# Two adapter and feed-forward layers on one core: 8-bit integers carried as signed fp16 multiples of 2^-24 in place of offset 16-bit integers

## The chip, the cores and the metric

The kernel runs on one core of one Trainium2 chip. The metric is the time of one execution on the device, in microseconds (us), lower is better. The engines are called as the profile calls them: PE is TensorE (PEld its weight loads), DVE is VectorE, ACT is ScalarE, POOL is GpSimd, SP is SyncE, which only issues DMAs here. Each engine works off its own queue in order, and the queues are tied together by semaphores.

## What is computed

x is 8 batches x 512 tokens x 256 channels. Two layers follow each other, both with a residual:

```python
x = x + ffn0(cond0(x, itok_B_0_8))     # adapter of the batch's language, LayerNorm, gamma, beta
x = x + ffn1(cond1(x, itok_B_0_7))     # linear layer of the batch's subject

def bitlinear(x, W, b):                # both feed-forward parts use it twice, 256 -> 1024 -> 256
    w_scale = clip(mean(abs(W)), 1e-5)
    Wq = clip(round(W / w_scale), -1, 1) * w_scale                 # ternary weights
    x_scale = clip(max(abs(x), axis=-1), 1e-5)                     # per token
    xq = clip(round(x * (127 / x_scale)), -128, 127) * (x_scale / 127)
    return xq @ Wq.T + b

ffn0 = bitlinear(gelu(bitlinear(x, W1, b1)), W2, b2)
ffn1 = bit_linear(silu(depthwise_conv1d(bit_linear(x, w1), conv_w, conv_b)), w2)   # conv over 3 tokens
```

So four times per token a row is divided by its own largest magnitude, rounded to integers within -127 to 127, and multiplied by a matrix of -1, 0 and 1. The product is an exact integer sum, and the two scales are multiplied in afterwards.

## The kernel before

**Tiling.** A batch is four tiles of 128 tokens (two pairs). All loops are unrolled. The queue of each engine is an order written out by hand: `first()` holds the first layer for all batches and the beginning of the second, `slot2(s)` repeats for the steady part of the second layer (one batch of it per slot), and `ending()` closes. No queue is sorted by anything else, so an instruction that is late holds up everything behind it on its engine.

**First layer, per pair or tile.** PE multiplies the adapter (`adapter_in`, `adapter_out`), DVE adds, centres and normalises and takes the largest magnitude of z (`absmax_z`, `scale_z`, `inverse_z`), ACT rounds z (`round_z`, L622), the result is transposed, PE multiplies by the ternary weights (`up1`, L1428) and adds the bias as one more matmul of the bank, ACT applies GELU (`gelu`, L639), DVE takes the largest magnitude (`absmax1`, L1128), POOL rounds (`round1`, L885), an SP DMA transposes, PE multiplies back to 256 channels (`down1`, L1451), and DVE or ACT apply the scales.

**Second layer, per batch.** PE transposes x and multiplies the subject's matrix (`linear`, L1491), ACT rounds y (`round_y`, L666), a DMA transposes, PE multiplies up (`up`, L1526), DVE applies the scales (`dequant`, L1179), and ACT, POOL and DVE each compute one of the three taps of the convolution (`last_tap` L686, `middle_tap` L939, `first_tap` L1191), POOL adds them (`tap_sum`, L949), PE transposes (`transpose_conv`), ACT applies SiLU (`silu`, L697), DVE takes the largest magnitude (`absmax2`, L1197), ACT rounds three tiles of four and POOL one (`round2`, L704 and L957), a DMA transposes, PE multiplies down (`down2`, L1578), and the scales and the residual end it.

**The integers' form.** The transposing DMA moves 16-bit elements. ACT or POOL compute value x scale + 128 and write it as uint16, so that the write rounds to an integer of 1 to 255. PE reads these 16 bits as fp16, where the bit pattern n of a small integer is the number n x 2^-24. What PE sums is therefore (q + 128) x 2^-24, and the 128 has to be taken out again, for each of the four products in another way:

- z, batches 2 to 7 (batches 0 and 1 are transposed on PE in another form): `low_row` (L1404) multiplies a row of -128 x 2^-24 by the weights, `bias_units` (L1071) adds it to the bias in those units (`bias9u`), and `up1` uses `bias9u` in the bias matmul (L1432).
- GELU's output: POOL adds up the columns of the down weights (`column_sums(1)`, L910, L912, L915), and each `down1` ends in a ninth matmul of `uncode` by `colsum` (L1452) behind its eight.
- y: `low_columns` (L1513) makes 8 columns, `low_copy` (L1185) moves them out of PSUM, and `dequant` (L1179) adds one to the bank before it multiplies by the token scales: a scalar_tensor_tensor with a pointer scalar, 64 times.
- SiLU's output: `column_sums(3)` and a ninth matmul (L1579) in each `down2`, apart from the two last tiles of batch 7, which are written in a wider form and turned on PE.

The factor 2^24 is put back by the small products on POOL (`scale_of_up1`, `scale_of_down1`, `spread_of_up`, `scale_of_down`).

Of the kernel before, what the change touches and what calls it, by code (L numbers as in the profile page):

```python
# [22 lines left out]
CODE = 128.0  # L23
# [5 lines left out]
def build_program(nc, t):  # L29
# [14 lines left out]
    with ExitStack() as ctx:  # L44
# [29 lines left out]
        uncode = sb("uncode", [P, P], BF16)  # L74
        colpart = sb("colpart", [P, 4, D], BF16)
        colsum = {n: sb(f"colsum{n}", [P, D], BF16) for n in (1, 3)}
# [55 lines left out]
        bias9u = sb("bias9u", [P, H], BF16)  # L132
        pick0 = sb("pick0", [P, P], BF16)
# [8 lines left out]
        r1 = [sb(f"r1_{k}", [P, H], U16) for k in range(TB)]  # L142
# [75 lines left out]
        s_pick = sem("s_pick")  # L218
        s_low0 = sem("s_low0")
        s_bias9u = sem("s_bias9u")  # L220
# [12 lines left out]
        s_colpart = sem("s_colpart")  # L233
        s_wround = sem("s_wround")
        s_wclip = sem("s_wclip")
        s_colsum = sem("s_colsum")
# [18 lines left out]
        ry = sb("ry", [P, TB, D], U16)  # L255
        ryT = [sb(f"ryT{k}", [P, TB, KD, P], U16) for k in range(2)]
        low_up = sb("low_up", [P, KH])
# [65 lines left out]
        p_low = sem("p_low")  # L323
        p_lowe = sem("p_lowe")
        p_pad = sem("p_pad")
        s_uncode = sem("s_uncode")
# [42 lines left out]
        def tile(b, j):  # L369
            return TB * b + j + 1  # L370
# [24 lines left out]
        def _(sp):  # L395
# [28 lines left out]
            def transpose1(b, j):  # L424
                sp.wait_ge(s_r1[j], b + 1)
                wait(sp, s_dn, tile(b - 1, j))
                sp.dma_start_transpose(q1T[j][:, :, :].bitcast(U16), r1[j][:, :]).then_inc(s_q1T[j], 16)
# [17 lines left out]
            def transpose2(b, k):  # L445
# [4 lines left out]
                sp.dma_start_transpose(q2T[k][:, :, :], r2[k][:, :]).then_inc(p_q2T[k], 16)  # L450

            def transpose_y(b):
# [4 lines left out]
                                       ry[:, :, :].rearrange("p k d -> p (k d)")).then_inc(p_yT, 16)  # L457
# [70 lines left out]
        def _(act):  # L528
# [85 lines left out]
            def round_z(b, p):  # L614
# [5 lines left out]
                for k in range(2):  # L620
                    o = rz[:, k, :] if b < Z0 else zq[p][:, KD * k:KD * (k + 1), :].rearrange("p n c -> p (n c)")
                    ins = act.activation(o, z[p][:, k, :], ACT.Copy, scale=qsz[p][:, k:k + 1],  # L622
                                         bias=ROUND if b < Z0 else CODE)
# [17 lines left out]

            def round1(b, j):
                act.wait_ge(s_qs1, tile(b, j))
                wait(act, s_q1T[j], 16 * b)
                act.activation(r1[j][:, :], g1[j % 2][:, :], ACT.Copy, scale=qs1[j % 2][:, 0:1],
                               bias=CODE).then_inc(s_r1[j], 1)

# [51 lines left out]
            def round2(b, k):  # L699
# [4 lines left out]
                act.activation(r2[k][:, :], silu_out(b, k), ACT.Copy, scale=qs2[k][:, 0:1],  # L704
# [1001 lines left out]
```

## Time and profile before

| | us |
|---|---|
| median of three runs | 294.62 (293.48 to 294.82) |
| the profiled execution | 293.92 |
| its span, first to last instruction | 292.0 |
| mean granted TensorE clock | 0.97 of full speed |

The span is what the rows below divide up; 1.9 us of the profiled execution lie around it. Busy times count every instruction of an engine once; matmuls are pipelined and their ends are modelled, so that a busy PE isn't PE at its peak. Read first how full each engine is in each stretch, then what ended the idle time of the one that leads there. An engine that is full in a stretch, without idle time, sets the pace of that stretch if its own work doesn't wait for a later engine.

### The profile page before, as it was taken

The page shows a single profiled execution, that of the slowest core. Times are in us where ns is not written, and L with a number is a line of the kernel's source. Part 1 is how long each engine was busy: PE and PEld are TensorE (multiplying, and loading weights), DVE is VectorE, ACT ScalarE, POOL GpSimd, SP SyncE. Part 2 cuts the span into 40 slices and gives each one's busy share as a digit, 9 for nine tenths or more (in the row PEclk, how much of TensorE's full clock was granted, in tenths as well). Part 3 has the DMA queues.
Part 4 walks back from the last instruction along what each step waited for, and adds up shares of the span by engine and source line. Part 5 has one row for each costly group of instructions (what it writes and reads, how often), then busy time and mean ns, then how long its engine had stood idle before and what let it go on. Part 6 is the DMA issues. An engine that isn't in the chain of part 4 may idle for free.

```text
span 292.0 us, 6500 instructions
## 1 busy us (share of the span) xinstructions
PE 265.6 (91%) x1762; PEld 192.5 (66%) x1774; DVE 255.2 (87%) x616; ACT 236.2 (81%) x396; POOL 260.2 (89%) x377
## 2 busy tenths in 40 slices
PE   6739999999999999999989989999999999969895
PEld 6516666556665576666667867686877868746794
DVE  0369998888999999868999999999999999999773
ACT  2199999997886884785669979989899898989780
POOL 4359999989899899899999999999999999999871
PEclk9755999999999999999999999999999999999999
DMA  5994788986656754595411525266482633943383
GB/s 156 306 312 125 236 251 249 247 165 177 164 117 158 163 101 108 117 165 126 111 33 37 114 60 129 64 104 148 114 176 77 111 73 72 182 110 92 90 217 110
DMA packets 104870, 41.37 MB, mean 142 GB/s; under 512 B 89157, under 2 KB 102265, under 8 KB 104834
## 3 DMA queue, kind: packets, MB, share of 16 engines
q1 hardware_dynamic: 98384, 32.86, 50.1%
q10 hardware_dynamic: 6450, 8.10, 8.7%
q8 instruction: 15, 0.25, 0.4%
q14 instruction: 21, 0.17, 0.2%
HBM read 16.04 MB, written 4.19 MB: 69 GB/s over the span
## 4 chain that ended last, share of the span: by engine, by line
PE 29%; POOL 28%; issue 19%; DVE 8%; ACT 8%; DMA 4%; SPq 2%; POOLq 0%; ACTq 0%; DVEq 0%
PE banks L1491 6%; POOL raw_all L949 5%; POOL r L885 5%; PE banks L1451 4%; PE banks L1526 3%; PE banks L1549 3%; DMA raw_all<-in_w1a 3%; PE banks L1428 3%; DVE raw_all L1191 2%; POOL mid L939 2%; PE banks L1578 2%; POOL raw_all L813 2%; DVE apad L1179 2%; POOL xs L854 2%; DVE am L1197 1%
## 5 line engine op out<-in xcount | busy, mean ns | idle before, releaser
L949 POOL TENSOR_TENSOR raw_all<-raw_all,mid 128x1024 f32<-128x1024 f32 (+1 forms) x31 | 55.3, 1785 | 0.0
L686 ACT ACTIVATE banks<-apad,taps 128x512 f32<-128x512 f32 x64 | 44.4, 700 | 6.2 <-DVE apad L1179 6.0
L1191 DVE SCALAR_TENSOR_TENSOR raw_all<-apad,taps,banks 128x512 f32<-128x512 f32 x64 | 46.8, 740 | 0.7 <-ACT banks L686 0.2
L1179 DVE SCALAR_TENSOR_TENSOR apad<-banks,low_up,dqb 128x512 f32<-128x512 f32 x64 | 46.4, 743 | 0.3 <-PE banks L1526 0.2
L1128 DVE TENSOR_REDUCE am<-g 128x1 f32<-128x1024 f32 x32 | 38.8, 1212 | 5.1 <-ACT g L639 5.0
L939 POOL TENSOR_SCALAR mid<-apad,taps,convb 128x512 f32<-128x512 f32 x56 | 42.4, 763 | 0.0
L639 ACT ACTIVATE g<-banks,dqz 128x1024 f32<-128x1024 f32 x32 | 35.5, 1110 | 8.0 <-PE banks L1432 4.4
L1197 DVE TENSOR_REDUCE am<-g 128x1 f32<-128x1024 f32 x30 | 36.2, 1207 | 2.1 <-ACT g L697 2.1
L885 POOL TENSOR_SCALAR r<-g,qs 128x1024 uint16<-128x1024 f32 x32 | 35.8, 1119 | 2.3 <-DVE qs L1140 1.8
L1526 PE MATMUL banks<-ryT,tern 128*128 128x512 f16 x128 | 35.9, 379 | 2.1 <-DVE raw_all L1191 1.9
L697 ACT ACTIVATE g<-banks 128x1024 f32<-128x1024 f32 x30 | 30.7, 1024 | 6.3 <-PE banks L1555 5.0
L1491 PE MATMUL banks<-wl,x2T 128*128 128x256 f32 x128 | 32.9, 386 | 1.9 <-issue 0.9
L1451 PE MATMUL banks<-tern,q1T 128*128 128x256 bf16 x256 | 33.2, 272 | 1.2 <-ACT down L652 1.0
L1549 PE MATMUL banks<-id,raw_all 128*128 128x128 f32 x220 | 29.8, 275 | 4.8 <-ACT g L697 4.8
L1549 PEld LDWEIGHTS banks<-id,raw_all 128*128 128x128 f32 x220 | 24.8, 141 | 11.2 <-ACT g L697 7.1
L1578 PE MATMUL banks<-tern,q1T 128*128 128x256 bf16 x240 | 31.2, 273 | 0.9 <-ACT down_out L722 0.5
L1451 PEld LDWEIGHTS banks<-tern,q1T 128*128 128x128 f16 x256 | 24.4, 98 | 11.1 <-issue 5.2
L1491 PEld LDWEIGHTS banks<-wl,x2T 128*128 128x128 f32 x128 | 22.2, 190 | 10.5 <-issue 6.2
L1578 PEld LDWEIGHTS banks<-tern,q1T 128*128 128x128 f16 x240 | 22.4, 98 | 7.9 <-ACT down_out L722 3.7
L1428 PE MATMUL banks<-tern,zqT 128*128 128x512 bf16 x87 | 26.6, 379 | 0.8 <-DMA zqT<-zq 0.3
L704 ACT ACTIVATE r<-g,qs 128x1024 uint16<-128x1024 f32 x21 | 24.2, 1153 | 0.2
L1379 PE MATMUL banks<-cw,hT 65*128 65x256 f32 x64 | 19.1, 427 | 3.9 <-ACT hT L598 3.3
(162 smaller groups left out, 615.5 us busy)
## 6 DMA issues: line engine op xcount, KB each, us to landing
xs<-in_x ACTq DMA_DIRECT2D x7, 512.0 KB, 3.6
out_y<-xs SPq DMA_DIRECT2D x14, 256.0 KB, 2.5
x2T<-in_xT ACTq DMA_DIRECT2D x4, 512.0 KB, 3.6
wl<-in_cwl SPq DMA_DIRECT2D x8, 256.0 KB, 3.0
xT<-in_xT ACTq DMA_DIRECT2D x3, 512.0 KB, 6.2
cw<-in_cw SPq DMA_DIRECT2D x16, 64.0 KB, 4.3
raw_all<-in_w1a SPq DMA_DIRECT2D x1, 1024.0 KB, 7.7
raw_all<-in_w2a SPq DMA_DIRECT2D x1, 1024.0 KB, 6.2
```

Source lines behind the costliest of these rows:

```text
L686: act.activation(bank(BANK_U[g % 3]), apad[:, f, 2:S + 2], ACT.Copy, scale=taps[:, f, 2:3]).then_inc(p_last, 1)
L885: pool.tensor_scalar(r1[j][:, :], g1[j % 2][:, :], qs1[j % 2][:, 0:1], CODE, ALU.mult, ALU.add) \
L939: pool.tensor_scalar(middle(b, f), apad[:, f, 1:S + 1], taps[:, f, 1:2], convb[:, f:f + 1], ALU.mult, ALU.add).then_inc(p_mid, 1)
L949: pool.tensor_tensor(c[:, 2 * q:2 * q + n, :], c[:, 2 * q:2 * q + n, :], mid[q % 2][:, 0:n, :], ALU.add).then_inc(p_sum, 1)
L1179: dve.scalar_tensor_tensor(out=apad[:, f, 1:S + 1], in0=bank(BANK_U[(KH * b + f) % 3]), scalar=low_up[:, f:f + 1], in1=dqb[b % 2][:, :], o ...
L1191: dve.scalar_tensor_tensor(out=conv[b % 2][:, f, :], in0=apad[:, f, 0:S], scalar=taps[:, f, 0:1], in1=bank(BANK_U[(KH * b + f) % 3]), op0= ...
L1197: dve.tensor_reduce(am2[k][:, :], silu_out(b, k), AX_X, ALU.max, apply_absolute_value=True) \
L1451: pe.matmul(o, q1T[j][:, c, :].bitcast(F16), w_dn0[:, c, :], start=(c == 0), stop=False)
L1491: pe.matmul(bank(bank_y(b, k))[:, a * D:(a + 1) * D], x2T[:, 2 * k + a, j, :], wl1[par][:, j, :], start=(j == 0), stop=False)
L1526: ins = pe.matmul(bank(BANK_U[g % 3]), w_up1[:, k, f * P:(f + 1) * P], ryT[b % 2][:, :, k, :].bitcast(F16), start=(k == 0), stop=(k == KD ...
L1549: pe.transpose(bank(bank_c(b, k) + f // KT)[:, (f % KT) * P:(f % KT + 1) * P], conv[b % 2][:, f, k * P:(k + 1) * P], id32[:, :])
L1578: pe.matmul(o, q2T[k][:, f, :].bitcast(F16), w_dn1[:, f, :], start=(f == 0), stop=False)
```

## The change

ACT and POOL now write the rounded values as fp16: value x scale, where the scale is 2^-24 of the former one, so that the value is q x 2^-24 with its sign and the fp16 write rounds to a multiple of 2^-24. There is no offset, and everything that took it out is dropped. The scale's factor sits in the small DVE instructions that form it (1/127 becomes 1/(127 x 2^-24)), and the small POOL products no longer multiply by 2^24. The transposing DMAs move the same bits.

Left out: the two `column_sums` (three POOL instructions each), `low_row` (4 matmuls), `bias_units` (2 DVE instructions), `low_columns` (16 matmuls of one column), `low_copy`, the ninth matmul of 32 `down1` and of 30 `down2`, five memsets at the start, and the waits on all of these. `dequant` becomes a tensor_tensor without the scalar. The order of everything else in every queue is unchanged.

```diff
-        r1 = [sb(f"r1_{k}", [P, H], U16) for k in range(TB)]
+        r1 = [sb(f"r1_{k}", [P, H], F16) for k in range(TB)]
...
-        ry = sb("ry", [P, TB, D], U16)
+        ry = sb("ry", [P, TB, D], F16)
...
                     ins = act.activation(ry[:, 2 * k + a, :], bank(bank_y(b, k))[:, a * D:(a + 1) * D], ACT.Copy,
-                                         scale=qsy[:, 2 * k + a:2 * k + a + 1], bias=CODE)
+                                         scale=qsy[:, 2 * k + a:2 * k + a + 1])
...
-                pool.tensor_scalar(r1[j][:, :], g1[j % 2][:, :], qs1[j % 2][:, 0:1], CODE, ALU.mult, ALU.add) \
+                pool.tensor_scalar(r1[j][:, :], g1[j % 2][:, :], qs1[j % 2][:, 0:1], 0.0, ALU.mult, ALU.add) \
...
-            def column_sums(n):
-
-                w = w_dn0 if n == 1 else w_dn1
-                pool.wait_ge(s_tern[n], 1)
-                wait(pool, s_colsum, n // 2)
-                pool.tensor_tensor(colpart[:, :, :], w[:, 0:4, :], w[:, 4:8, :], ALU.add).then_inc(s_colpart, 1)
...
-                dve.scalar_tensor_tensor(out=apad[:, f, 1:S + 1], in0=bank(BANK_U[(KH * b + f) % 3]),
-                                         scalar=low_up[:, f:f + 1], in1=dqb[b % 2][:, :],
-                                         op0=ALU.add, op1=ALU.mult).then_inc(p_a, 1)
...
+                dve.tensor_tensor(apad[:, f, 1:S + 1], bank(BANK_U[(KH * b + f) % 3]), dqb[b % 2][:, :], ALU.mult) \
+                    .then_inc(p_a, 1)
...
                 o = bank(BANK_DN)[:, k * D:(k + 1) * D]
                 for c in range(KH):
-                    pe.matmul(o, q1T[j][:, c, :].bitcast(F16), w_dn0[:, c, :], start=(c == 0), stop=False)
-                ins = pe.matmul(o, uncode[:, :], colsum[1][:, :], start=False, stop=True)
+                    ins = pe.matmul(o, q1T[j][:, c, :].bitcast(F16), w_dn0[:, c, :], start=(c == 0), stop=(c == KH - 1))
                 ins.then_inc(s_dn, 1)
```

## Rows read from the trace of the kernel before

**Rows 1.** Page, part 1: busy time, share of the span and instructions of each engine.

```profile
PE 265.6 (91%) x1762; PEld 192.5 (66%) x1774; DVE 255.2 (87%) x616; ACT 236.2 (81%) x396; POOL 260.2 (89%) x377
```

**Rows 2.** Page, part 4: the chain that ended last, shares by engine.

```profile
PE 29%; POOL 28%; issue 19%; DVE 8%; ACT 8%; DMA 4%; SPq 2%; POOLq 0%; ACTq 0%; DVEq 0%
```

**Rows 3.** Stretches of the span: from:to and length, then busy time (instructions) per engine, clock.

```profile
30.00:70.00 40.00, 37.65 (x237) 24.48 (x240) 36.14 (x115) 39.82 (x70) 36.65 (x69) 1.00 0.85 225
70.00:115.00 45.00, 43.10 (x280) 28.30 (x284) 43.72 (x132) 34.10 (x70) 40.10 (x85) 1.00 0.61 138
115.00:155.00 40.00, 38.31 (x232) 26.25 (x235) 33.96 (x75) 26.66 (x44) 38.74 (x51) 1.00 0.53 108
155.00:268.00 113.00, 106.17 (x745) 81.14 (x744) 111.28 (x222) 102.80 (x161) 113.00 (x118) 1.00 0.50 106
268.00:292.00 24.00, 19.43 (x173) 16.70 (x170) 15.19 (x31) 14.63 (x21) 15.14 (x18) 0.99 0.51 132
```

**Rows 4.** Timeline of DVE: start, length; the reciprocal of y's scales in two successive batches.

```profile
212.69 0.18 DVE L1171 RECIPROCAL qsy<-sy 128x4 f32<-128x4 f32 x1
...
230.65 0.18 DVE L1171 RECIPROCAL qsy<-sy 128x4 f32<-128x4 f32 x1
```

**Rows 5.** Timeline of POOL, the same two batches: the scales' product.

```profile
214.68 0.25 POOL L920 TENSOR_SCALAR dqy<-sy,ws 128x4 f32<-128x4 f32 x1
...
231.91 0.26 POOL L920 TENSOR_SCALAR dqy<-sy,ws 128x4 f32<-128x4 f32 x1
```

**Rows 6.** Groups by form: line, operation, count; busy us, mean ns; idle before: work removed.

```profile
L910 POOL TENSOR_TENSOR colpart<-tern 128x1024 bf16<-128x1024 bf16 x2 | 4.3, 2129 | 0.0
...
L912 POOL TENSOR_TENSOR colpart<-colpart 128x512 bf16<-128x512 bf16 x2 | 2.3, 1160 | 0.2
...
L915 POOL TENSOR_TENSOR colsum<-colpart 128x256 bf16<-128x256 bf16 x2 | 1.3, 672 | 0.2
...
L1071 DVE SCALAR_TENSOR_TENSOR bias9u<-bias9b,banks 128x512 bf16<-128x512 bf16 x2 | 1.3, 679 | 0.0
...
L1404 PE MATMUL banks<-tern,pick 128*128 128x512 bf16 x4 | 1.0, 377 | 0.1
...
L1185 DVE COPY low_up<-banks 128x8 f32<-128x8 f32 x1 | 0.2, 158 | 0.0
```

**Rows 7.** Timeline of PE: a down projection's ninth matmul and what follows.

```profile
161.69 0.27 PE L1452 MATMUL banks<-colsum,uncode 128*128 128x256 bf16 x1
161.80 0.93 PE L1549 MATMUL banks<-id,raw_all 128*128 128x128 f32 x7
```

**Rows 8.** Groups by form: VectorE's product and sum, with and without a pointer scalar.

```profile
L1179 DVE SCALAR_TENSOR_TENSOR apad<-banks,low_up,dqb 128x512 f32<-128x512 f32 x64 | 46.4, 743 | 0.3 <-PE banks L1526 0.2
...
L1104 DVE SCALAR_TENSOR_TENSOR z<-zg,rstd,banks 128x256 f32<-128x256 f32 x32 | 13.9, 476 | 0.3 <-ACT zq L622 0.2
...
L1084 DVE SCALAR_TENSOR_TENSOR xx<-banks,xs 128x256 f32<-128x256 f32 x16 | 6.1, 420 | 6.2 <-PE banks L1379 6.2
```

**Rows 9.** Groups by form: roundings to 16 bits, and one to f32.

```profile
L885 POOL TENSOR_SCALAR r<-g,qs 128x1024 uint16<-128x1024 f32 x32 | 35.8, 1119 | 2.3 <-DVE qs L1140 1.8
...
L704 ACT ACTIVATE r<-g,qs 128x1024 uint16<-128x1024 f32 x21 | 24.2, 1153 | 0.2
...
L962 POOL TENSOR_SCALAR raw_all<-raw_all,qs 128x512 f32<-128x512 f32 x2 | 1.4, 696 | 0.0
```

**Rows 10.** One line's instructions in a stretch: L1452, the ninth matmul of the first layer.

```profile
115.00:155.00 40.00, 2.45 (x9) 0.88 (x9) 1.00 0.53 108
```

**Rows 11.** One line's instructions in a stretch: L1179, the dequantisation of the second layer.

```profile
155.00:268.00 113.00, 37.04 (x52) 1.00 0.50 106
```

**Rows 12.** Chain that ended last, 264:292: first and last of five ninth matmuls in it.

```profile
276.81 0.11 PE banks L1579
...
285.97 0.11 PE banks L1579
```

**Rows 13.** Page, part 2: TensorE's granted clock in 40 slices, tenths of full.

```profile
PEclk9755999999999999999999999999999999999999
```

More of the change, by code:

```diff
@@ L640, in gelu @@
                                scale=dqz[p][:, j % 2:j % 2 + 1]).then_inc(s_gelu, 1)
[L642 to L646, printed above, removed]
             def dequant_down1(b, k):
@@ L798, in _ @@
             pool.memset(qc[:, :, :, :], 0.0)
-            def scale_rows():
-                for k in range(2):
-                    ins = pool.memset(zq_scales(k), 0.0)
-                ins.then_inc(s_pick, 1)
-                pool.wait_ge(s_pick, 1)
-                for k in range(2):
-                    pool.memset(zq_scales(k)[:, :, 0:1, 0:1], 1.0)
-                pool.memset(pick0[:, :], 0.0).then_inc(s_pick, 1)
-                pool.wait_ge(s_pick, 2)
-                pool.memset(pick0[:, 0:1], -CODE * UNIT).then_inc(s_pick, 1)
+            for k in range(2):
+                pool.memset(zq_scales(k), 0.0)
             def clipped_weights(n):
@@ L1065, in bias_last @@
                 dve.tensor_tensor(bias9b[96:P, :], b1rest[96:P, :], bias9b[96:P, :], ALU.subtract).then_inc(s_b1, 1)
-            def bias_units():
-                dve.wait_ge(s_low0, 1)
-                for m in range(2):
-                    h = slice(m * 512, (m + 1) * 512)
-                    ins = dve.scalar_tensor_tensor(out=bias9u[:, h], in0=bias9b[:, h], scalar=UNIT,
-                                                   in1=bank(BANK_UP + m), op0=ALU.mult, op1=ALU.add)
-                ins.then_inc(s_bias9u, 1)
             def add_adapted(b, p):
@@ L1397, in transpose_z @@
                 ins.then_inc(s_zT, 1)
-            def low_row():
-                pe.wait_ge(s_pick, 3)
-                pe.wait_ge(s_gelu, tile(Z0 - 1, 2))
-                for m in range(2):
-                    for c in range(KD):
-                        ins = pe.matmul(bank(BANK_UP + m), pick0[:, :], w_up0[:, c, m * 512:(m + 1) * 512],
-                                        start=(c == 0), stop=(c == KD - 1))
-                ins.then_inc(s_low0, 1)
             def up1(b, j):
@@ L1428, in up1 @@
                         pe.matmul(o, q, w_up0[:, c, m * 512:(m + 1) * 512], start=(c == 0), stop=False)
-                    if b < Z0:
-                        ins = pe.matmul(o, qcT[p][:, k, :], bias9b[:, m * 512:(m + 1) * 512], start=False, stop=True)
-                    else:
-                        ins = pe.matmul(o, zqT[p][:, 2 * KD + k, :].bitcast(BF16), bias9u[:, m * 512:(m + 1) * 512],
-                                        start=False, stop=True)
+                    c = qcT[p][:, k, :] if b < Z0 else zqT[p][:, 2 * KD + k, :].bitcast(BF16)
+                    ins = pe.matmul(o, c, bias9b[:, m * 512:(m + 1) * 512], start=False, stop=True)
                 ins.then_inc(s_up, 1)
@@ L1505, in spread_scales @@
                 ins.then_inc(p_bc, 1)
-            def low_columns():
-                pe.wait_ge(s_tern[2], 1)
-                pe.wait_ge(s_uncode, 1)
-                pe.wait_ge(s_qT, PAIR * Z0)
-                for f in range(KH):
-                    for k in range(KD):
-                        ins = pe.matmul(bank(2)[:, f:f + 1], w_up1[:, k, f * P:(f + 1) * P], uncode[:, 0:1],
-                                        start=(k == 0), stop=(k == KD - 1))
-                ins.then_inc(p_low, 1)
             def up(b, f):
@@ L1577, in down2 @@
                     for f in range(KH):
-                        pe.matmul(o, q2T[k][:, f, :].bitcast(F16), w_dn1[:, f, :], start=(f == 0), stop=False)
-                    ins = pe.matmul(o, uncode[:, :], colsum[3][:, :], start=False, stop=True)
+                        ins = pe.matmul(o, q2T[k][:, f, :].bitcast(F16), w_dn1[:, f, :], start=(f == 0), stop=(f == KH - 1))
                 ins.then_inc(p_dn[k], 1)
```

85 lines of the change are left out of this document (28 added, 57 removed).

## The prediction, made before the changed kernel had run

> **What bounds the kernel now.** I read the page's part 1 first [rows 1]: PE 91%, POOL 89%, DVE 87% and ACT 81% of the span. No engine leads by enough to name it from an average, and the chain [rows 2] gives PE and POOL 29 and 28%, so different stretches have different limits. The stretches [rows 3] show them. Their columns are PE, PEld, DVE, ACT and POOL busy, then the clock, the DMA share and GB/s.
>
> - 30 to 70 us: ACT is busy 39.82 of 40.00. POOL has 3.35 idle, DVE 3.86. ACT sets the pace.
> - 70 to 115: DVE is busy 43.72 of 45.00, POOL only 40.10, ACT 34.10. DVE sets the pace.
> - 115 to 155, the change of layers: POOL 38.74 and PE 38.31 of 40.00, DVE 33.96. PE and POOL lead together.
> - 155 to 268, the steady second layer: POOL 113.00 of 113.00 and DVE 111.28. Which of the two leads is seen from their period, not from their share. DVE's y reciprocal comes back after 230.65 - 212.69 = 17.96 us [rows 4], POOL's product for the same two batches after 231.91 - 214.68 = 17.23 [rows 5]. POOL is full because it works off a backlog (2.0 us behind DVE in one batch, 1.3 in the next). DVE is the limit.
> - 268 to 292, the tail: every engine falls under 64% apart from PE (19.43 of 24.00). PE's down projections follow each other in the chain [rows 12].
>
> **The change, part by part.** The sum is made against the span of 292.0 us, stretch by stretch, because a removed instruction counts only where its engine leads.
>
> *Column sums on POOL.* One costs 2.13 + 1.16 + 0.67 = 3.96 us [rows 6], two 7.9. The first runs while ACT is the full engine, where ACT's queue doesn't shrink by a single instruction: ACT can gain at most its idle 0.18 us up to 70 us. DVE then has 1.28 us of idle time to lose up to 115 us. So whatever POOL wins, all up to 115 us is worth at most 0.18 + 1.28 plus what DVE itself drops there, the 0.16 us copy [rows 6], hence 1.6. Below it is nothing. I take 0.8, the middle, since part of such idle time is the handing over of semaphores. `bias_units` (2 x 0.68 us, [rows 6]) and `low_row` (4 matmuls of 512 columns, 4 x 0.38 us even if nothing overlapped) lie before 70 us, beside the full ACT: nothing. The five memsets run at the start where nothing waits for POOL: nothing. If ACT's and DVE's cover were not there, the first column sum would count in full, 4.0; that is a rival below. The second falls in the change of layers, where PE is nearly as full as POOL: its price is what PE then allows, next.
>
> *The ninth matmuls on PE.* Its record says 0.27 us, but it overlaps: the next group starts 161.80 - 161.69 = 0.11 us after it [rows 7]. In 115 to 155 there are 9 [rows 10]: 9 x 0.11 = 1.0. With the second column sum gone POOL has 1.3 + 4.0 us of slack there, so PE leads alone and could also win back some of its own 1.69 us of idle time: 0 to 1.7. I take 0.4, as most of PE's idle is waiting for ACT and DVE. Sum 1.4, from 1.0 to 2.7. In 155 to 268 the ninth matmuls lie beside DVE's work: nothing, and if DVE weren't the limit, 23 x 0.11 = 2.5. In the tail five are in the chain: 5 x 0.11 = 0.55 [rows 7, 12], and 0.3 if a wait for DVE or ACT comes in between two of them.
>
> On the same matmuls the Trainium skill speaks against the change ("Perfetto Trace Analysis", section Identifying the Most-Contended Engine): matmul busy time is a bad measure of a full PE, the share of weight loads a better one. That share is 26.25 of 40.00 us in 115 to 155 [rows 3], which would make PE no limit, the PE terms 0 and the sum 3.7 in place of 5.6. The rows show the opposite in the small, a next group that starts directly behind the ninth matmul [rows 7].
>
> *Dequantisation on DVE.* 64 scalar_tensor_tensor with a pointer scalar, 743 ns each [rows 8], become tensor_tensor without one. The trace has no such tensor_tensor of f32 out of PSUM. The nearest rows are the same operation at 256 elements with a pointer scalar (476 ns) and with a constant (420 ns) [rows 8]: 56 ns less, hence 687. A second neighbour, 512 elements and a constant scalar, took 679 [rows 6]: 64 less. The other bound is that nothing is saved, since the operation might cost the same whatever its operands are. A loss has no reason: one tensor from PSUM and one from SBUF are read as before. I take 56 ns. 52 of the 64 lie in 155 to 268 [rows 11], where DVE leads: 52 x 0.056 = 2.9, from 0 to 3.3. DVE's period becomes 17.96 - 8 x 0.056 = 17.5, still above POOL's 17.23, so POOL is next at a distance of 0.3 us per batch and isn't reached. The 12 earlier ones lie where PE leads: nothing.
>
> *The roundings.* ACT and POOL write fp16 in place of uint16. No row shows an fp16 write by POOL. POOL's write of f32 took 696 ns for 512 elements and of uint16 1119 for 1024 [rows 9], which is 423 ns for 512 more elements: the output's type doesn't show. The same holds on ACT, 1153 ns for 1024 [rows 9]. I take zero; the upper bound is the first rival. The additions of 0.0, the changed constants and the products on POOL keep their instructions and their number: nothing. The DMAs move the same bytes, and SP's queue loses only waits.
>
> **Sum.** 0.8 + 1.4 + 2.9 + 0.55 = 5.65 us, span 286.35. The profiled execution took 293.92 and would take 288.3; it lies 0.70 under the median of 294.62, so against that median it is 289.0. The low ends give 0 + 1.0 + 0 + 0.3 = 1.3 us (293.3), the high ends 1.6 + 2.7 + 3.3 + 0.6 = 8.2 (286.4).
>
> **The rivals.**
> 1. *The fp16 write is slow (slower).* The values are tiny, multiples of 2^-24, and POOL might handle such a write in more steps. If a rounding took twice its 1.12 us, the 32 of the first layer cost 36 us more on POOL, against its idle 3.35 + 4.90 + 1.26 = 9.5 up to 155 us [rows 3] and the 7.9 removed: 18 us. In the second layer one rounding per batch takes 1.1 us more against a slack of 0.3, over 113 / 17.96 = 6.3 batches another 5. With the 5.6 gained elsewhere partly void: about 312. It decides from (9.5 + 7.9) / 32 = 0.54 us per rounding. Against it: [rows 9].
> 2. *The clock falls (slower).* In the first slices the granted clock is 5 tenths, the 1.2 GHz level, with PE busy less densely, and from the fifth on 9 [rows 13]. If PE with less work fell to it in the tail, at least the 9.2 us from the first to the last ninth matmul of the chain [rows 12] and at most the 19.4 us that PE is busy there [rows 3] would be added: between them, 289.0 + 14 = 303. It needs a PE that stands idle much more. In 155 to 268 it is idle 6.8 of 113 us, and the change adds 2.5. The Trainium skill ("TensorE: Matmul & The Clock Gate", section Why this matters for your kernels) warns of drops after idle gaps; the clock of 1.00 in the stretches up to 268 us [rows 3] agrees that these gaps cause none so far.
> 3. *tensor_tensor costs as much as before (still faster).* 2.9 falls away: 291.9. With PE's idle time not recovered, 292.3.
> 4. *Nothing visible (same).* The hand-made order is coupled so tightly that each gain ends in the next wait: only the tail and some 0.5 us remain, 293.6.
> 5. *The chain means what it says (faster).* POOL has 28% of it [rows 2]. If ACT's and DVE's fullness is partly a matter of their place behind POOL, the first column sum counts 4.0 in place of 0.8: 285.8.
>
> **How the numbers follow.** The forecast, 286.8 to 291.2, has 0.57; rival 5 and below 0.13; rival 3 with its surroundings, 291.2 to 293.1, 0.14; rival 4 0.08; rival 1 0.05; rival 2 0.03. A change of 0.5% (1.5 us) is about what a measurement of this kernel can tell from none. Faster by more, under 293.1: 0.57 + 0.13 + 0.14 = 0.84. Same: 0.08. Slower: 0.08. The range goes from 284.8, a microsecond under rival 5, to 293.0: above lie 0.16, below 0.04.
>
> **What would show it.** The removed groups are gone; `dequant` at about 687 ns; roundings on POOL at 1119 and on ACT at 1153. ACT still full in 30 to 70 us, with POOL showing some 4 us more idle time there. The distance of the y reciprocals at 17.5. POOL no longer 100% busy in the second layer, without its backlog. The tail shorter by 0.5. What would make me wrong: a `dequant` at 740 takes 2.9 away; a batch period under 17.4 would mean that POOL or something else paced DVE; a first layer shorter by 3 us or more would mean that ACT's fullness was no limit.

## The result, and the profile after

The change makes the kernel slower by 0.8%. In two comparisons, each on one chip side by side, the ratio to the kernel before is 1.0077 (95% interval 1.0041 to 1.0114; medians 296.75 and 294.05) and 1.0078 (1.0047 to 1.0108; 297.08 and 294.21). The forecast was 289.0 with a range up to 293.0. The runs of the changed kernel fall into two groups: 3 of the 12 of the second comparison took 294.4 to 294.6, the other 9 took 296.0 to 298.7. The kernel before has no such groups (292.6 to 295.5).

Two executions of the changed kernel were profiled: one of 294.70 us (span 292.9), called *after*, and one of 298.67 (span 296.8), the second trace. Busy time by engine in *after*, to be laid beside [rows 1]:

```profile
PE 259.5 (89%) x1680; PEld 186.0 (63%) x1692; DVE 251.4 (86%) x613; ACT 236.2 (81%) x396; POOL 253.5 (87%) x366
```

PE lost 6.1 us of work, DVE 3.8, POOL 6.7, and the time didn't fall. The stretches of [rows 3], the same columns:

```profile
30.00:70.00 40.00, 36.05 (x227) 23.61 (x229) 33.71 (x109) 38.40 (x67) 31.52 (x62) 1.00 0.85 214
70.00:115.00 45.00, 41.73 (x250) 26.07 (x253) 43.93 (x132) 34.21 (x72) 40.56 (x87) 1.00 0.68 140
115.00:155.00 40.00, 37.92 (x227) 25.64 (x228) 33.82 (x78) 27.35 (x44) 35.64 (x51) 1.00 0.52 108
155.00:268.00 113.00, 104.15 (x722) 78.71 (x720) 109.98 (x223) 103.56 (x163) 113.00 (x117) 1.00 0.49 106
268.00:292.00 24.00, 18.18 (x161) 15.63 (x159) 14.05 (x30) 13.54 (x19) 15.05 (x18) 1.00 0.62 132
```

Two things are wrong against the forecast. From 30 to 70 us ACT isn't full any more (38.40 in place of 39.82), though nothing was added: something makes it wait. And from 155 to 268 POOL still shows 113.00 of 113.00.

The prices were right. Groups by form, with count, busy us and mean ns, beside [rows 9, 11]:

```profile
L1128 DVE TENSOR_TENSOR apad<-banks,dqb 128x512 f32<-128x512 f32 x64 | 42.6, 683 | 0.3 <-PE banks L1443 0.2
L856 POOL TENSOR_SCALAR r<-g,qs 128x1024 f16<-128x1024 f32 x32 | 36.0, 1124 | 4.3 <-DVE qs L1091 3.7
L685 ACT ACTIVATE r<-g,qs 128x1024 f16<-128x1024 f32 x21 | 24.2, 1153 | 0.1
```

`dequant` takes 683 ns in place of 743 (forecast 687), an fp16 write on POOL 1124 ns and on ACT 1153, as the uint16 writes did. The distance of DVE's y reciprocals, forecast at 17.5 us, is 17.85.

**Where the time goes.** The start of the same instruction was compared over the traces. Each number is how much later (+) or earlier (-) it starts than in the trace of before, in us:

| start in the trace of before | after | second trace |
|---|---|---|
| 46.24, DVE `absmax1` | -0.38 | -0.35 |
| 54.74, DVE `absmax1` | +0.69 | +5.19 |
| 115.47, DVE `absmax1` | +0.41 | +4.81 |
| 187.91, POOL `add2` | -0.35 | +3.99 |
| 248.60, DVE y reciprocal | -0.67 | +3.69 |
| 281.22, POOL `add2` | -0.11 | +4.26 |
| 283.60, POOL's last `add2` | +0.91 | +4.88 |
| span | +0.8 | +4.8 |

The loss is made in two places, 46 to 55 us (1.1 and 5.5 us) and 281 to 284 us (1.0 and 0.6). In between, up to 281 us, 0.8 and 0.9 us are won.

**46 to 55 us.** Idle time from 44 to 62 us in the second trace: who waited for whom, us in total, times, longest:

```profile
ACT mid L550 <- DMA raw_all<-in_w2b: 3.3, 1, 3.3
PE banks L1279 <- ACT mid L550: 2.7, 1, 2.7
DVE am L1079 <- ACT g L626: 2.5, 1, 2.5
```

ACT's `weight_sum(3)` waits for the load of the fourth weight, w2b, and everything behind it in ACT's queue waits too, then PE, then DVE. The load's own row (KB, us from issue to landing), before and in the second trace:

```profile
raw_all<-in_w2b SPq DMA_DIRECT2D x1, 1024.0 KB, 7.2
...
raw_all<-in_w2b SPq DMA_DIRECT2D x1, 1024.0 KB, 10.7
```

The stretches around it in the second trace, and the middle one in the trace of before:

```profile
41.00:44.00 3.00, 3.00 (x20) 2.25 (x19) 2.54 (x7) 2.96 (x4) 2.64 (x6) 1.00 1.00 326
44.00:46.00 2.00, 1.48 (x9) 1.24 (x8) 1.59 (x7) 1.88 (x5) 0.43 (x3) 1.00 2.82 172
46.00:48.00 2.00, 2.00 (x16) 1.15 (x15) 2.00 (x9) 0.00 (x0) 0.00 (x0) 1.00 0.07 25
50.00:56.00 6.00, 4.76 (x17) 2.67 (x18) 1.62 (x6) 6.00 (x12) 2.53 (x6) 0.56 1.18 267
...
46.00:48.00 2.00, 2.00 (x12) 1.12 (x11) 2.00 (x5) 1.96 (x2) 1.84 (x3) 1.00 1.10 353
```

The last column is GB/s: the DMA engines move 326, then 25 for two microseconds, where they moved 353 before. The trace's packets show why: 19 of them, of the SP and the ACT queue alike, start between 44.8 and 45.3 us and take up to 3.9 us. I call this the stall. PE then idles, and from 50 to 56 us its granted clock is 0.56 of full speed, near the 1.2 GHz level: an `up1` matmul pair takes 1.01 us in place of 0.59. The wait was 3.3 us and the loss 5.5; where PE's clock stayed at 1.00 through such a stall (before121 below), a wait of 2.7 us cost 2.7.

### The profile page after: what moved, and what is told of

Same layout as the page of the kernel before. It is cut to its first block, busy times and chain, and to the rows that moved or that the text cites. A ratio compares the mean times of both kernels' runs of the same rounds, so it can differ in the third digit from the quotient of the medians.

```text
span 292.9 us, 6314 instructions
## 1 busy us (share of the span) xinstructions
PE 259.5 (89%) x1680; PEld 186.0 (63%) x1692; DVE 251.4 (86%) x613; ACT 236.2 (81%) x396; POOL 253.5 (87%) x366
## 4 chain that ended last, share of the span: by engine, by line
PE 37%; issue 16%; ACT 13%; POOL 12%; DVE 10%; DMA 7%; SPq 3%; ACTq 1%; DVEq 0%; POOLq 0%
PE banks L1418 10%; PE banks L1443 5%; PE banks L1466 4%; POOL r L856 3%; PE banks L1380 3%; ACT r L685 2%; ACT g L678 2%; DVE raw_all L1135 2%; PE banks L1495 2%; DMA raw_all<-in_w1a 2%; PE banks L1362 2%; ACT ry L647 2%; DMA cb<-in_cb 2%; DMA q1T<-r 2%; PE banks L1396 2%
## 5 line engine op out<-in xcount | busy, mean ns | idle before, releaser
L1079 DVE TENSOR_REDUCE am<-g 128x1 f32<-128x1024 f32 x32 | 38.8, 1213 | 6.6 <-ACT g L626 6.4
L1128 DVE TENSOR_TENSOR apad<-banks,dqb 128x512 f32<-128x512 f32 x64 | 42.6, 683 | 0.3 <-PE banks L1443 0.2
L856 POOL TENSOR_SCALAR r<-g,qs 128x1024 f16<-128x1024 f32 x32 | 36.0, 1124 | 4.3 <-DVE qs L1091 3.7
L1141 DVE TENSOR_REDUCE am<-g 128x1 f32<-128x1024 f32 x30 | 36.2, 1208 | 3.1 <-ACT g L678 3.1
L1418 PEld LDWEIGHTS banks<-wl,x2T 128*128 128x128 f32 x128 | 22.2, 190 | 10.9 <-issue 6.5
L685 ACT ACTIVATE r<-g,qs 128x1024 f16<-128x1024 f32 x21 | 24.2, 1153 | 0.1
```

The costliest lines, as they stand in the source:

```text
L856: pool.tensor_scalar(r1[j][:, :], g1[j % 2][:, :], qs1[j % 2][:, 0:1], 0.0, ALU.mult, ALU.add) \
L1079: dve.tensor_reduce(am1[j % 2][:, :], g1[j % 2][:, :], AX_X, ALU.max, apply_absolute_value=True) \
L1128: dve.tensor_tensor(apad[:, f, 1:S + 1], bank(BANK_U[(KH * b + f) % 3]), dqb[b % 2][:, :], ALU.mult) \
L1418: pe.matmul(bank(bank_y(b, k))[:, a * D:(a + 1) * D], x2T[:, 2 * k + a, j, :], wl1[par][:, j, :], start=(j == 0), stop=False)
```

## The experiments

Each run was timed in rounds beside the kernel before on the same chip; the ratio is to that, with its 95% interval.

### Which part holds the loss

The change falls into four parts, one for each rounded value, and each can be made alone.

**again** is the changed kernel once more (the second trace above): 1.0078.

> The changed kernel once more, beside the four parts. If its loss is a property of the kernel, the ratio to the kernel before is 1.005 to 1.011 again (about 296 against 294). If it was chance, the ratio is within 0.997 to 1.003. A second trace also tells whether the stall of the transposes in the tail (q1T, 5.3 us from issue to landing) belongs to the kernel: then it is there again; if it is chance, the transposes of the tail land in about 2.8 us.

The loss belongs to the kernel, and so does a late tail: the landing of the tail's transpose was late again.

**only_y**: the y part in the kernel before.

```diff
-                dve.scalar_tensor_tensor(out=apad[:, f, 1:S + 1], in0=bank(BANK_U[(KH * b + f) % 3]),
-                                         scalar=low_up[:, f:f + 1], in1=dqb[b % 2][:, :],
-                                         op0=ALU.add, op1=ALU.mult).then_inc(p_a, 1)
+                dve.tensor_tensor(apad[:, f, 1:S + 1], bank(BANK_U[(KH * b + f) % 3]), dqb[b % 2][:, :], ALU.mult) \
+                    .then_inc(p_a, 1)
```

> The kernel before with the change made for y alone: fp16 ry, dequant as a tensor_tensor without the scalar, low_columns and low_copy gone; everything else keeps its offset. Theory A (the prediction's step, DVE leads the second layer by its period): 2.9 us less, 291.2, ratio 0.990. Theory B (POOL's queue, without a gap from 137 to 276 us, sets the second layer, and 64 shorter dequants only make DVE wait more): ratio 0.998 to 1.002, POOL 113.0 busy of 113 in 155 to 268 as before, DVE's busy time there 1.3 us less.

0.9994 (0.9970 to 1.0018). The forecast gave this part 2.9 us; it gives nothing that can be measured. POOL stayed at 113.00 of 113.00, as theory B says, and the y reciprocals kept their distance of 17.95 us. The profiled execution was the longest of the twelve (297.41): it lost 2 us at 60 us to a short stall of the DMAs that its kernel doesn't have as a rule, since the median is that of before.

**only_g** and **only_s**: the GELU part and the SiLU part, each with its column sum and its ninth matmuls gone.

```diff
-                ins = pe.matmul(o, uncode[:, :], colsum[1][:, :], start=False, stop=True)
...
-                    ins = pe.matmul(o, uncode[:, :], colsum[3][:, :], start=False, stop=True)
```

> The kernel before with the change made for GELU's output alone: round1 in fp16, column_sums(1) and the ninth matmul of down1 gone. The prediction: 0.8 us at the column sum and about 1 at the matmuls in 115 to 155, ratio 0.994. Theory B: the second layer's POOL queue begins after the first layer, whose last stretch is set by dequant(0,0) and PE, so at most 0.5 us come through: 0.998 to 1.0. Theory C (the loss of the whole change sits at 46 to 77 us, where the first layer starts up, and comes with the freed 3.96 us of POOL, after which transposes and loads are issued in another mix): ratio 1.003 or more.

> The kernel before with the change made for SiLU's output alone: round2 in fp16, column_sums(3) and the ninth matmul of down2 gone. The prediction: 0.55 us in the tail plus what the second column sum gives, ratio 0.997. Theory B: the column sum is covered (POOL then waits for dequant(0,0)), the tail gives 0.5: 0.998. Theory D (the loss sits in the tail, where two transposes meet a store on SP's queue once down2 is shorter): ratio 1.002 or more, with q1T's landing over 4 us at 277 to 283.

1.0004 (0.9978 to 1.0030) and 0.9987 (0.9966 to 1.0009). Neither holds the loss.

**only_z** and **no_z**: the z part alone, and all but the z part.

> The kernel before with the change made for z alone: fp16 zq, low_row, bias_units and their waits gone, and of the start's memsets those of pick0 and of the 1.0 in the scale rows. By now the loss of the whole change is located: in the second trace of the changed kernel (298.67) everything up to 46 us is 0.35 us early, then w2b's load lands 10.7 us after its issue in place of 7.2, ACT waits 3.3 us for it in its queue, PE stands idle 2.7 us, its clock is granted at 0.50 from 52 to 56 us, and from 60 us on everything is 5.1 us late. Theory E (the loads of the start meet in another way because the start runs earlier): the z part holds it, ratio 1.004 or more and runs that split in two clusters. Theory F (the freed 4 us of POOL at 44 to 48 us do it): ratio 0.997 to 1.001.

> The whole change but the z part: GELU's, y's and SiLU's rounding in fp16, low_row, bias_units and all memsets of the start as in the kernel before. Theory E: 0.996 to 1.0, one cluster. Theory F: 1.005 to 1.009 as the whole change.

1.0002 (0.9980 to 1.0024) and 0.9987 (0.9961 to 1.0013). So neither theory as it stood: no part holds the loss, and of the combinations that were run only the whole change does.

### The stall is made by where a block of POOL's code is loaded

**writes**: the changed kernel with the five memsets of the start kept. The expectation says that 0.14 us of them stand ahead of the bias memset; as run, all five stand behind it.

```diff
+            pool.memset(uncode[:, :], -128.0 * UNIT)
             for k in range(2):
-                pool.memset(zq_scales(k), 0.0)
+                ins = pool.memset(zq_scales(k), 0.0)
+            ins.then_inc(s_pick, 1)
+            pool.wait_ge(s_pick, 1)
+            for k in range(2):
+                pool.memset(zq_scales(k)[:, :, 0:1, 0:1], 0.0)
+            pool.memset(pick0[:, :], 0.0).then_inc(s_pick, 1)
+            pool.wait_ge(s_pick, 2)
+            pool.memset(pick0[:, 0:1], -128.0 * UNIT).then_inc(s_pick, 1)
```

> The changed kernel with the five memsets of the start kept, at their places and with their waits, writing tiles that nothing reads (0.14 us of them stand ahead of the memset that the bias load waits for). Theory E in its narrowest form (these writes alone set how the first loads meet): 0.997 to 1.001. Theory E in a wider form (z's other parts do it as well) or F: 1.005 to 1.009.

0.9981 (0.9957 to 1.0005): five writes of tiles that nobody reads take the loss away. **layout** (the six old tiles declared and unused) and **rewrites** (five more memsets, on existing tiles) ask what about them does it: the places of the tiles, or POOL's work.

```diff
...
+        bias9u = sb("bias9u", [P, H], BF16)
+        pick0 = sb("pick0", [P, P], BF16)
...
+            pool.memset(qc[:, 0, :, :], 0.0).then_inc(s_pick, 1)
+            pool.wait_ge(s_pick, 2)
+            pool.memset(qc[:, 1, :, :], 0.0)
```

> The changed kernel with the six tiles that it no longer needs (uncode, colpart, colsum, bias9u, pick0, low_up) declared again at their places and never touched, so that every other tile lies where it lay in the kernel before. The first weight's load lands 6.4 to 6.6 us after its issue in the four traces without the start's extra memsets and 7.6 to 8.8 in the six with them; the stall at 45 us was seen in three of those four and in none of the six. If the tiles' places decide that, 0.996 to 1.0 and one cluster. If POOL's writes at the start do, 1.005 to 1.009 as the changed kernel.

> The changed kernel with five more memsets and their two waits at the start, which write zeros once more to tiles that exist (qc and the scale rows), so that no tile moves. If POOL's writes (their time, their instructions) decide, 0.996 to 1.0. If the tiles' places do, 1.005 to 1.009.

layout 1.0068 (1.0037 to 1.0100), rewrites 0.9968 (0.9938 to 0.9997). Not the places. That left POOL's writes, their time, or the number of its instructions. The DMA records have a queue of kind "instruction" with packets of 8 KB, and one of them moves with POOL's instructions and with nothing else:

| kernel | code packet at, us | packets of the first transpose, us | w2b issued at | landed after | ratio |
|---|---|---|---|---|---|
| before | 36.1 | 39.0 to 40.0 | 39.06 | 7.2 | 1 |
| only_z | 38.0 | 38.6 to 39.6 | 38.70 | 7.1 | 1.0002 |
| writes | 37.4 | 40.0 to 41.1 | 40.16 | 7.1 | 0.9981 |
| rewrites | 35.4 | 38.3 to 39.4 | 38.44 | 7.1 | 0.9968 |
| after, again | 38.9, 39.0 | 38.4 to 39.8 | 38.47, 38.50 | 8.5, 10.7 | 1.0078 |
| layout | 40.6 | 39.9 to 41.3 | 39.97 | 10.8 | 1.0068 |
| relief (below) | 38.8 | 38.3 to 39.7 | 38.37 | 10.9 | 1.0093 |

Where the packet comes 0.4 to 0.6 us behind the issue of w2b's load, the load is late; where it comes ahead, it is late in none of these. One later trace, spread's, is an exception: the load landed after 8.3 us with the packet at 36.8, and 0.6 us were lost. There a 16 KB code packet of PE came at 46.2 us, and 256-byte packets of a transpose beside it took up to 1.7 us.

The third column gives another reading of the same rows. The first transpose (`q1T<-r`, issued just ahead of w2b) moves 1024 packets of 256 bytes. They start within 1.1 us where the code packet lies outside them, and within 1.4 to 1.5 us in the four traces where it falls among them (after, again, layout, relief), which are the four with a late load. w2b's own packets start only 1.5 us or more after that code packet has ended. So what the code packet meets may be the transpose and not the load; w2b_early, below, bears on this.

A rule of the Trainium skill stands beside this, "Advanced Engine Details and Errata", section ISA Cache: code is cached in lines of 16 KB, 256 instructions. The 16 KB packets of the other instruction queue agree, they move with PE's program (**pad**, below); POOL's come in 8 KB here, so 128 instructions of 64 bytes, and the measurement decides. Four runs tested it with memsets of one column, which write a tile of their own: 12 and 128 of them in the changed kernel, 116 and 121 in the kernel before.

```diff
+            for k in range(12):
+                pool.memset(fill[:, k:k + 1], 0.0)
```

> The changed kernel with 12 memsets of one column each at the end of POOL's start (a tile of its own, no waits, some 25 ns each by the four constants' memsets at 0.25 to 0.33 us, in 8.7 us in which POOL idles). What the traces have shown by now: in the four kernels with the stall an 8 KB packet of an instruction queue comes at 38.8 to 40.6 us, 0.4 to 0.8 us behind the issue of w2b's load, in the eight without it at 35.4 to 38.0, ahead of that issue; only POOL's number of instructions moves it. Theory H (it is POOL's code, and fetching it in the middle of that load makes the stall): the packet comes near 36 us, no stall, 0.995 to 0.999. Rival (the time or the data of the kept memsets did it): 1.005 to 1.009.

> The same with 128 memsets of one column (some 3 us of POOL's idle time at the start), the number of 64-byte instructions in 8 KB. Theory H: the block boundary lies where it lay in the changed kernel, the packet comes at 38.5 to 40 again, the stall is back: 1.004 to 1.009. Rival (more work of POOL at the start, of whatever kind, is what helps): 0.995 to 0.999.

code12 0.9962 (0.9940 to 0.9985), code128 1.0006 (0.9984 to 1.0029), on the same chip: medians 293.58 and 295.06. Whether the packet is in the window where it was expected is seen in the DMA queues (packets, MB, share) and the row of the load, first code12 in 35 to 38 us, then code128 in 38 to 41:

```profile
q14 instruction: 1, 0.01, 0.6%
...
raw_all<-in_w2b SPq DMA_DIRECT2D x1, 1024.0 KB, 7.0
...
q14 instruction: 1, 0.01, 1.2%
...
raw_all<-in_w2b SPq DMA_DIRECT2D x1, 1024.0 KB, 9.0
```

Both as theory H has it: 12 instructions move the packet to 36.2 us and the loss is gone, 128 bring it back to 39.5 and ACT waits 1.6 us for w2b. That is no later than w2b's issue at 39.49, but among the packets of the transpose (39.4 to 41.0). The loss came back only in part, 1.5 us of 3.4.

> The kernel before, whole, with 116 memsets of one column at the end of POOL's start: 128 less the 12 or so instructions by which the changed kernel's POOL program is shorter up to 40 us. Theory H: the packet moves to about 39 us, w2b lands 8 to 11 us after its issue, and the kernel before, with nothing of the change in it, loses what the changed one lost: 1.004 to 1.010. If the stall needs the changed kernel's other timing, 0.998 to 1.002.

before116 missed its place: the packet came at 45.1 us, and the ratio was 1.0004 (0.9985 to 1.0023). The count of 12 included the column sum, whose instructions lie behind this block's border; only seven, five memsets and two waits, lie ahead of it.

> The kernel before, whole, with 121 memsets of one column at the end of POOL's start in place of 116. With 116 the code packet came at 45.1 us, too late to meet anything (ratio 1.0004). Five more instructions ahead of the boundary move it back to some 39 us, to where the changed kernel has it. Theory H (this packet behind the issue of w2b's load is enough): w2b lands 8.5 to 11 us after its issue in place of 7.2, 1 to 5 us are lost between 46 and 55 us, ratio 1.003 to 1.010. If the changed kernel's other timing is needed too: 0.998 to 1.002.

1.0147 (1.0099 to 1.0195). The kernel before, with none of the change in it, loses at least as much as the changed kernel did, and the kernel with five memsets fewer loses nothing. The traced execution (296.89) is near the fastest of the six, which go up to 301.26; what the slower ones lose on top wasn't traced. Its DMA rows in 38 to 41 us, the load, its waits and the stall:

```profile
q14 instruction: 1, 0.01, 1.0%
...
raw_all<-in_w2b SPq DMA_DIRECT2D x1, 1024.0 KB, 10.1
...
ACT mid L566 <- DMA raw_all<-in_w2b: 2.7, 1, 2.7
...
46.00:48.00 2.00, 2.00 (x10) 1.15 (x10) 2.00 (x6) 0.36 (x1) 1.84 (x3) 1.00 0.42 27
```

The same 27 GB/s at the same place. In the kernel before, the block's position alone makes the loss. **w2b_early** takes the load away from under the packet:

```diff
-                load_table(); load_weights(2); transpose1(0, 0); load_weights(3); transpose1(0, 1); load_adapter(4)
+                load_table(); load_weights(2); load_weights(3); transpose1(0, 0); transpose1(0, 1); load_adapter(4)
```

> The changed kernel with one edit in SP's order: w2b's load is issued right behind w1b's, near 28 us, ahead of the first transpose. POOL's program is as in the changed kernel, so the code packet stays at some 39 us, but w2b has landed by 40. Theory H, second half (the packet does harm only because it meets this load): no stall, ratio 0.995 to 0.999, unless the earlier load delays the tokens' loads at 33 to 35 us, which would show as ACT or DVE waiting there. If the stall is not tied to w2b: 1.004 to 1.009.

0.9981 (0.9948 to 1.0015), w2b issued at 27.58, the packet at 38.7. A stall is still there, earlier and with nobody waiting for it: 98 GB/s in 41 to 44 us, where before has 328, and ACT busy 2.96 of 3.00 in it. Part of the difference is that w2b's load isn't there any more, but 2048-byte packets of the ACT queue take up to 1.9 us in it:

```profile
41.00:44.00 3.00, 2.86 (x17) 2.14 (x15) 2.17 (x7) 2.96 (x6) 2.02 (x3) 1.00 1.06 98
```

In this trace the stall comes without w2b's load too, and costs little because nobody waits for a load in it. The second half of theory H is thus wrong as it was put: the load is what makes the stall costly, not what makes it. The code packet at 38.7 again fell among the first transpose's packets (37.6 to 39.6), as in all seven traces with this stall (after, again, layout, relief, code128, before121, w2b_early) and in none of the other thirteen. Spread's, with PE's packet, is among the thirteen. This is read from traces alone; no run set the packet clear of the transpose and behind w2b's issue, or the other way round. How a packet that itself takes 0.3 to 0.6 us holds up all others some 3 to 7 us later isn't seen in these traces and stays open.

### What the second layer is limited by

**relief** takes POOL's small products off it.

```diff
-                act.activation(dqb[b % 2][:, :], bank(bank_x(b)), ACT.Copy).then_inc(p_bce, 1)
+                act.activation(dqb[b % 2][:, :], bank(bank_x(b)), ACT.Copy, scale=ws[:, 2:3]).then_inc(p_bce, 1)
...
-                pool.tensor_scalar(dq2[p][:, :], s2[p][:, :], ws[:, 3:4], 0.0, ALU.mult, ALU.add) \
-                    .then_inc(p_dq2, 1)
+                act.activation(dq2[p][:, :], s2[p][:, :], ACT.Copy, scale=ws[:, 3:4]).then_inc(p_dq2, 1)
```

> The changed kernel with POOL's small products of the second layer taken off POOL: ws is multiplied in where ACT copies the spread scales (no instruction more), and scale_of_down moves to ACT. POOL has 0.26 + 2 x 0.26 = 0.78 us less per batch, 5 us in 155 to 268. Theory B (POOL's unbroken queue is the limit of the second layer): POOL shows idle time there, DVE becomes the limit at a period of about 17.5, and the time falls by 2 to 4 us against the changed kernel: 293 to 295 where that has 297, its fastest runs at about 291.5 in place of 294.4. Rival (DVE or ACT already set the pace): no change, or slower by up to 1 us, since ACT gets 1 us more per batch.

1.0093 (1.0069 to 1.0117): it has the stall, and so says little. **pad** is writes with 48 more instructions in PE's program; **best** is pad with relief; **spread** is pad with the first half of relief alone, which adds nothing to ACT but a scale.

```diff
             def keep_busy(i):
+                if 6 <= i <= 9:
+                    for _ in range(10):
+                        pe.matmul(bank(BANK_DN)[:, 0:P], idb[:, :], idb[:, :], start=True, stop=True)
+                    return
```

> The kernel of the run with the start's memsets kept, and in it four of the keep_busy calls (numbers 6 to 9, 0.3 us per matmul before) done by ten bf16 matmuls each in place of two f32 ones: about the same time on PE, 48 instructions more in PE's program. Traces so far: a 16 KB packet of an instruction queue falls at 277.3 us in four of the changed kernels and lasts up to 1.8 us, the tail's transposes then land late, and the tail loses 0.6 to 1.0 us between 281 and 284 us; in the kernel before it falls at 283.5. Theory G (PE's program is fetched in blocks of 256 instructions, and the block fetched at 277.3 meets the transpose): the packet moves to about 274.5 and the tail's loss goes, 0.6 to 1.0 us less than the memset kernel, 0.995. Rival (the fetch is another engine's, or harmless): the packet stays at 277.3, 0.998.

> The memsets kept, POOL's small products of the second layer moved to ACT or folded in, and PE's instructions moved as in the run beside it. If the three effects add (no stall at 45 us; 0.3 to 0.7 us from POOL; 0.6 to 1.0 us from the tail), 292.4 to 293, ratio 0.993 to 0.996, faster than both kernels. If the DVE's period of 17.9 is all there is, 0.997.

> The kernel of the padded run (0.9962) with spread_of_up taken off POOL and nothing added elsewhere but the factor ws in ACT's copy of the spread scales (724 ns in place of 639, once per batch). POOL has 0.26 us per batch less, 2.1 us by 275 us; in the padded run DVE was 1.6 us early at 273 and POOL 0.85. Theory B (POOL's queue sets when the last batch is turned): 0.5 to 0.8 us less than the padded run, 292.5, 0.994. Rival (the loop over DVE, ACT and PE sets it as well, as it seems where scale_of_down went to ACT too): 0.996 to 0.998.

pad 0.9962 (0.9934 to 0.9991), best 0.9977 (0.9951 to 1.0004), spread 0.9959 (0.9938 to 0.9980). The second layer, 155 to 268 us, in pad, spread and best:

```profile
155.00:268.00 113.00, 104.56 (x724) 78.86 (x722) 110.22 (x219) 103.71 (x164) 113.00 (x118) 1.00 0.47 106
...
155.00:268.00 113.00, 103.91 (x719) 78.49 (x718) 109.30 (x220) 103.45 (x161) 111.65 (x112) 1.00 0.46 104
...
155.00:268.00 113.00, 103.53 (x717) 78.13 (x715) 109.46 (x222) 104.95 (x173) 108.86 (x100) 1.00 0.49 106
```

POOL has idle time as soon as it is relieved (1.35 and 4.14 us), but nothing gets faster: the last three distances of the y reciprocals are 17.85, 17.85 and 17.84 us in pad, 18.22, 17.95 and 17.94 in spread and 17.95, 18.10 and 17.95 in best. Theory B fits the kernels with the full POOL and doesn't say what comes next: the handing over between DVE, ACT and PE holds the distance near 17.9 whichever of DVE and POOL is relieved.

The traces narrow down which loop that is. The shorter `dequant` leaves the distance as it is: 17.95 in before and in only_y, 17.84 to 17.88 in only_s, which keeps the long one, and in *after*, which has the short one. DVE waits for ACT's `last_tap` instead, in 155 to 268 us of before and of *after*:

```profile
DVE raw_all L1191 <- ACT banks L686: 0.2, 1, 0.2
...
DVE raw_all L1135 <- ACT banks L667: 1.4, 5, 0.4
```

What goes with the distance is `down2`'s ninth matmul. Every trace that keeps it has 17.94 us or more. Those without it, and with ACT's copy of the spread scales as before, have 17.84 to 17.92, about the 0.11 us of one such matmul less. In relief, spread and best that copy takes 0.73 us in place of 0.64, and the distance is 17.93 or more again. This fits a loop through PE and ACT with one ninth matmul and that copy in it and without the time of `dequant`. No run tested it by itself.

**The tail.** In pad a 16 KB code packet moved from 277.3 to 274.5 us as expected, and the 0.9 us that writes lost between 281 and 284 us were gone (-0.83 and -0.82 us against before, in place of -0.16 and +0.70). The same matmuls of PE in before and in *after*, there with the wait ahead of them:

```profile
281.48 1.04 PE L1578 MATMUL banks<-tern,q1T 128*128 128x256 bf16 x8
...
282.64 1.03 PE L1495 MATMUL banks<-tern,q1T 128*128 128x256 bf16 x8 [1.23 <-DMA q1T<-r]
```

and SP's issue of the transpose that they wait for, before and *after*:

```profile
277.31 1.25 SPq L450 DMA_TRANSPOSE q1T<-r  x1
...
277.20 2.55 SPq L435 DMA_TRANSPOSE q1T<-r  x1
```

Over the 20 traces, a tail with a code packet of over 1.25 us at this transpose lost 0.4 to 1.0 us there, one whose packets stayed under 1.2 us at most 0.2. As times, pad and writes don't differ beyond their intervals, so this part is read from traces alone.

## Why the prediction was wrong

- **Up to 115 us, 0.8.** Right in kind, half the size. ACT hid the first column sum: from 30 to 70 us POOL's busy time fell from 36.65 to 31.52 and DVE's steps didn't come earlier. In code12, where no stall is in the way, 0.4 us were won from 76 to 115 us.
- **115 to 155 us, 1.4.** Half of it: from DVE's `absmax1` at 115 us to POOL's `add2` at 188 us, 0.6 and 0.7 us were won in code12 and pad. The second column sum was hidden as said; POOL now waits 3.2 us for `dequant(0,0)`.
- **155 to 268 us, 2.9. This step failed.** The duration was right, the limit wrong. I saw POOL 113.00 of 113.00, saw that its period over two batches was shorter than DVE's [rows 4, 5], and concluded that DVE's own work leads. Two things were wrong in this. DVE's period isn't its own work: eight dequantisations per batch, each 0.06 us shorter, left it at 17.95 in only_y, and in *after* it is 17.85 in place of the forecast 17.5. And a queue that is never empty is a limit all the same: POOL's last step of the stretch is its first one plus all its work, and what DVE gains only lengthens its lead. Against the trace of before, DVE in *after* ran ahead by up to 1.1 us and gave nearly all of it back at the end, where PE had to wait for POOL's last tap. The wait of PE in *after* from 268 to 280 us, then the last `absmax2` of the tail in before and in *after*:

```profile
PE banks L1466 <- POOL mid_last L897: 1.3, 1, 1.3
...
276.28 1.22 DVE L1197 TENSOR_REDUCE am<-g 128x1 f32<-128x1024 f32 x1 [1.22 <-ACT g L697]
...
276.17 1.22 DVE L1141 TENSOR_REDUCE am<-g 128x1 f32<-128x1024 f32 x1 [2.12 <-ACT g L678]
```

  The Trainium skill ("Perfetto Trace Analysis", section Identifying the Most-Contended Engine) says to take the engine with the highest occupancy and work on it first. The trace agrees with its first half, POOL it was; relieving POOL brought nothing either.
- **Tail, 0.55.** From POOL's `add2` at 281.22 to the end before took 10.82 us, only_s 10.50, pad 10.58 and spread 10.65: 0.2 to 0.3 won. Late transposes take more than that back, 11.77 in *after*.
- **The step that isn't there, the larger miss.** The prediction put the five memsets at nothing because they "run at the start where nothing waits for POOL". Their time is worth nothing, as it says. Their place in POOL's program isn't, and no term or rival was about the length of the programs. The change takes 164 matmuls and weight loads out of PE's program (1762 + 1774 to 1680 + 1692) and 11 instructions and some waits out of POOL's, so code is loaded at other moments. That is worth 1.0078 against 0.9962 (again and code12), 1.2% or 3.4 us. The change's own gain is the rest: 0.9962 in code12 and in pad, 1.1 us, a fifth of what was forecast.
- **The rivals.** Rival 2, the falling clock, happened at 50 to 56 us and not in the tail, as a follower of the stall. Rival 4, every gain ends in the next wait, was given 0.08 and describes the change itself. Rivals 1, 3 and 5 are refuted: fp16 writes cost what uint16 writes cost, tensor_tensor is cheaper, the first column sum is hidden.

A version that beats both kernels is the changed one with its code moved: code12 (0.9962), spread (0.9959), pad (0.9962) and rewrites (0.9968) all have intervals under 1.

## What to carry to other kernels

An engine that is full without a gap over a long stretch bounds when the stretch can end, even if its period looks shorter than another's: a shorter period with a backlog means that it is catching up, and the gain of the others is worth no more than the backlog. The engine with the longer period needn't be limited by its own work either; shorten its instructions alone, as only_y does, and see whether the period follows. Relieving the full engine may give nothing, as here. When a removed instruction costs time, look whether it moved the loading of code: compare the instruction queues' packets in both traces with the transposes and loads that somebody waits for, and test it with a few empty instructions in an idle stretch. A weight load whose wait stands in an in-order queue should be issued well ahead of its use.

## What the runs showed of the hardware

- In seven traces one 8 KB packet of POOL's code was loaded among the 256-byte packets of a DMA transpose. In five of them up to 3.5 us followed, about 6 us later, in which all queues together moved mostly 25 to 45 GB/s in place of over 300; *after* (1.5 us at 39 to 73 GB/s) and w2b_early (2 us at 36 to 71) had it weaker. Five memsets of one column in POOL's idle time decided between 1.0004 and 1.0147.
- PE's code comes in packets of 16 KB that took 0.9 to 2.1 us each, about one every 18 us in before. When one met a DMA transpose in the tail of *after*, SP's issue took 2.55 us in place of 1.25 and packets of 256 bytes up to 1.7 us (up to 2.3 in code12, at 96 us).
- A scalar_tensor_tensor on DVE with a pointer scalar took 743 ns, a tensor_tensor of the same operands 683, and the following instruction starts as much earlier (0.66 and 0.60 us after it).
- In the second trace PE had been idle for 2.7 us, and from 52 to 56 us its granted clock was 0.50, the 1.2 GHz level. In before121 it had been idle for 2.1 us, and the clock stayed at 1.00.
